# Orders for the whole run in place of periods, and groups of 2, 2, fourteen times 4, 2, 2 sequences

## What is computed

```python
x = x + _L0_xattn_ref(_layernorm(x), ctx, ...)   # 16 heads of 8: q, k, v, rms norm of q and k, softmax, values, projection
x = x + _L0_ffn_ref(_layernorm(x), ...)          # activations and weights rounded; 128 -> 512, convolution over 3 tokens, silu, 512 -> 128
x = x + _L1_xattn_ref(_layernorm(x), ctx, ...)   # one head of 128: softmax(bf . ctx) . ctx, joined with x, 256 -> 128
x = x + _L1_ffn_ref(_layernorm(x), ...)          # 8 experts of 256; every token is taken by every expert
# _L1_ffn_ref, where K = 128 tokens are taken of 128:
#   affinity = softmax(x @ gate_w);  h = silu(x @ Wg[e]) * (x @ Wu[e]);  x_out += affinity[e] * (h @ Wd[e])
```

## Time and profile before

| | us |
|---|---|
| median of 3 runs | 1228.7 |
| lowest, highest | 1226.46, 1229.22 |
| span of the profiled execution | 1219.6 |
| PE busy | 1100.5 |
| DVE busy | 984.3 |
| ACT busy | 826.6 |
| POOL busy | 682.8 |

### The profile page before, as it was taken

The page is one execution under the profiler, slowest core; times in us unless marked ns, Lnnn a source line. Parts: engine busy times, 40 slices in busy tenths (PEclk is TensorE's granted clock), DMA queues, the critical chain, the costliest instruction groups (busy, mean ns, idle before and its releaser), DMA issues.

```text
span 1219.6 us, 27479 instructions
## 1 busy us (share of the span) xinstructions
PE 1100.5 (90%) x9891; PEld 789.6 (65%) x9891; DVE 984.3 (81%) x2728; ACT 826.6 (68%) x1685; POOL 682.8 (56%) x827
## 2 busy tenths in 40 slices
PE   1677778999999899999999999999999998989998
PEld 1544555766767676767757676767767675767775
DVE  3668787989899898989898898989898897877653
ACT  1255375878768686768778686868778686868655
POOL 3212134566565747566575748475575747375775
PEclk9688898999999999999999999999999999999999
DMA  6120212121312113121212112130212022011000
GB/s 207 30 55 20 55 36 56 35 47 38 62 38 56 36 34 56 35 53 32 62 38 57 36 38 53 35 64 21 62 38 60 22 35 48 22 23 26 18 10 9
DMA packets 151396, 53.63 MB, mean 44 GB/s; under 512 B 116832, under 2 KB 150624, under 8 KB 150880
## 3 DMA queue, kind: packets, MB, share of 16 engines
q1 hardware_dynamic: 149248, 47.82, 17.7%
q10 hardware_dynamic: 2016, 4.08, 0.9%
HBM read 24.73 MB, written 4.19 MB: 24 GB/s over the span
## 4 chain that ended last, share of the span: by engine, by line
PE 72%; DVE 12%; SPq 5%; POOL 4%; issue 2%; ACT 2%; DMA 1%; POOLq 0%; DVEq 0%; ACTq 0%
PE py L750 16%; PE pa L601 5%; SPq L444 4%; PE pa L568 4%; PE pg L740 4%; PE pu L740 3%; PE pg L742 3%; PE pg L741 3%; PE pu L741 3%; PE pu L742 3%; PE pa L591 3%; DVE q_st L1155 2%; PE pa L608 2%; PE pb L648 2%; POOL xn L921 2%
## 5 line engine op out<-in xcount | busy, mean ns | idle before, releaser
L962 POOL TENSOR_TENSOR moe<-moe 128x512 f32<-128x512 f32 x256 | 336.3, 1318 | 293.7 <-ACT moe L897 147.8
L750 PE MATMUL py<-wd_s,moe 128*128 128x128 f32 x1856 | 248.7, 278 | 3.9 <-POOL moe L962 3.7
L750 PEld LDWEIGHTS py<-wd_s,moe 128*128 128x128 f32 x1856 | 231.7, 192 | 21.7 <-issue 7.8
L883 ACT ACTIVATE tg<-pg 128x512 f32<-128x512 f32 x232 | 139.7, 602 | 104.7 <-PE pg L742 104.0
L1155 DVE TENSOR_REDUCE q_st<-pa 128x4 f16<-128x480 f32 x256 | 168.4, 658 | 34.8 <-PE pa L568 33.6
L1307 DVE SCALAR_TENSOR_TENSOR moe<-tg,pg 128x512 f32<-128x512 f32 x232 | 157.3, 678 | 32.1 <-ACT tg L883 30.1
L897 ACT ACTIVATE moe<-pu 128x512 f32<-128x512 f32 x232 | 140.4, 605 | 33.7 <-PE pu L742 31.8
L817 ACT ACTIVATE probs<-pa 120x512 f32<-120x512 f32 x256 | 139.8, 605 | 22.3 <-PE pa L591 22.0
L568 PE MATMUL pa<-kbd,qht 128*128 128x480 f16 x256 | 96.4, 377 | 30.7 <-DVE q_st L1155 26.4
L740 PE MATMUL pg<-x4h,wg_h 128*128 128x512 f16 x232 | 88.6, 382 | 16.4 <-DVE moe L1307 16.4
L921 POOL TENSOR_SCALAR xn<-x,lnm,lnr 128x128 f32<-128x128 f32 x192 | 88.3, 473 | 5.2
(11 more groups left out here) (198 smaller groups left out, 2514.4 us busy)
## 6 DMA issues: line engine op xcount, KB each, us to landing
kbd<-kht SPq DMA_DIRECT2D x512, 3.8 KB
xin<-in_x SPq DMA_DIRECT2D x16, 256.0 KB, 2.8
xres<-in_x SPq DMA_DIRECT2D x16, 256.0 KB, 3.0
out_x<-acc SPq DMA_DIRECT2D x16, 256.0 KB, 3.2
ctxt_a<-in_ctx_t SPq DMA_DIRECT2D x16, 240.0 KB, 2.7
ctxt_b<-in_ctx_t SPq DMA_DIRECT2D x16, 240.0 KB, 2.9
ctxn_b<-in_ctx SPq DMA_DIRECT2D x16, 240.0 KB, 3.6
wd_s<-in_wd ACTq DMA_DIRECT2D x1, 1024.0 KB, 9.5
```

The source lines that it names most:

```text
L750: mm = pe.matmul(moe_y(g, e)[:, j, :], hu[:, u % 3, j * S:(j + 1) * S], wd_s[:, u, :], start=(half == 0 and j == 0), stop=(half == 1), ski ...
L883: act.activation(tg[:, u % 2, :], moe_bank("g", g, u)[:, :], ACT.Tanh, scale=0.5 / WSCALE).then_inc(tg_done.sem, 1)
L962: pool.tensor_tensor(hu[:, u % 3, :], gw[:, u % 3, :], us[:, u % 3, :], ALU.mult)\
```

## The change

- **Group sizes.** `SIZES` gives 18 groups: 0 and 1, and 16 and 17, have 2 sequences, the fourteen between them 4. `FIRST[g]` is a group's first sequence. Tiles keep their size; a small group uses the first half of each, so most of its instructions have 256 columns in place of 512. Semaphores that count sequences count by `FIRST` (`Signal.each`).
- **Whole-run orders.** `periods`, `TURNS` and `run_turns` go. `ORDER` has one string of letters per engine for the whole run, and `run` takes for each letter the next step of that stage, whatever the group. A stage of one group may begin between any steps of another.
- **Seven streams.** The max matmuls, their DVE maxima and the second kbd load are a stream of their own, **m**, so that they can run ahead of stage a, into the next group.
- **Finer steps.** q, k and v are three steps, the taps two, the rms and gate steps are single instructions of DVE's row, and POOL's layer norms are split into the roots (`roots`) and the four scalings (`normalise`).
- **kbd.** A small group also takes 32 DMAs, 16 for each of its two sequences.
- **Waits** that periods had made needless are written out, such as those for the last reads of x4h2, q_st2, qht2 and aff by the group two back.
- `UNREAD` is empty. `TAIL = 3` keeps the second banks for groups 15, 16 and 17.

```diff
 B, S, SC, D = 64, 128, 120, 128
-GB = 4
-NG = B // GB
+SIZES = (2, 2) + 14 * (4,) + (2, 2)
+GB = max(SIZES)
+NG = len(SIZES)
+FIRST = tuple(sum(SIZES[:g]) for g in range(NG))
...
-UNREAD = {
-    "wna": {2: 12, 6: 2, 9: 2, 10: 2, 11: 1, 14: 1, 19: 1, 22: 1, 24: 1, 29: 1, 32: 1, 36: 1, 41: 1, 44: 1, 45: 2, 49: 1, 50: 1, 52: 1},
...
+UNREAD = {}
+TAIL = 3
...
     def at(self, g, k=1):
-
-        return g * self.per + k
+        return g * self.per + FIRST[g] * self.each + k
...
-TURNS = {
...
+STAGES = "wnmabdc"
+ORDER = {
+    "sp": (
+        "annnnnnnnmnnnnannmnnbnnbnnmannndnbbnmnnanndncmnbbbnbnnnanmcdnbbbbnnnmannndbbbnbcannmnndnbbbbnnncamdnnnbbbbnn",
...
-            if g >= NG - 3 and u % 2:
+            if g >= NG - TAIL and u % 2:
...
+        def run(engine, do, between=None):
+
+            todo = {stage: iter([(step, g) for g in (range(NG) if stage != "w" else (0,))
+                                 for step in steps_of(engine, stage, g)]) for stage in STAGES}
+            for at, stage in enumerate("".join(ORDER[engine])):
                 if between is not None:
-                    between(kind, at)
-                step = next(steps[stage])
-                do[stage](step, groups[stage])
+                    between(at)
+                step, g = next(todo[stage])
+                do[stage](*step, g)
...
-            def load_kbd(g, half):
-
-                part = slice(2 * half, 2 * half + 2)
-                if later(g):
-                    sp.wait_ge(max_ps.sem, max_ps.at(g - 1, 4 * (2 * half + 2)))
-                for h in range(H):
+            def load_part(g, half):
+                part = slice(0, first_half(g)) if half == 0 else slice(first_half(g), size(g))
+                for h in range(H):
                     rows = slice(h * HD, (h + 1) * HD)
                     sp.dma_start(kbd[rows, part, h, :], kht[rows, part, 0:SC]).then_inc(kbd_in[half][h // HQ].sem, 16)
...
-                    o = moe_bank(what, g, u)
-                    pe.matmul(o[:, :], w_hi[:, us], x4h[:, :], start=True, stop=False)
+                    o = moe_bank(what, g, u)[:, 0:wide]
+                    pe.matmul(o, w_hi[:, us], x4h, start=True, stop=False)
...
-            def normalise(sig, at, n, src, dst):
-
-                pool.tensor_scalar(lnv[:, n, :], mv[:, n, :, 1], EPS_LN, 1.0, ALU.add, ALU.mult).then_inc(sig.sem, 1)
+            def roots(sig, at, i, n):
+
+                pool.tensor_scalar(lnv[:, i, 0:n], mv[:, i, 0:n, 1], EPS_LN, 1.0, ALU.add, ALU.mult).then_inc(sig.sem, 1)
```

More of the change, by code:

```diff
@@ L352, in build_program @@
-        n_steps = ["ln1", "xn1t", "qkv", "rms", "rms_k", "rms_q", "qkht"]
-        a_steps = [("max", 0, c) for c in range(4)]
-        a_steps.append(("stacks", 0))
-        for t in range(GB):
-            steps = [("scores", t, 0), ("max", t + 1, 0), ("scores", t, 1), ("values", t, 0), ("max", t + 1, 1),
-                     ("values", t, 1), ("max", t + 1, 2), ("max", t + 1, 3), ("turn", t), ("stacks", t + 1)]
-            a_steps += [step for step in steps if not (step[0] in ("max", "stacks") and step[1] == GB)]
@@ L359, in build_program @@
-        a_steps += ["ont", "proj"]
-        b_steps = ["ln2", "quant", "xit"]
-        for k in range(KB + 1):
-            steps = [("taps", k - 1), ("fc1", k), ("silu", k - 1)]
-            b_steps += [step for step in steps if 0 <= step[1] < KB]
-        b_steps += [(name, t) for t in range(GB) for name in ("h2t", "hit")] + ["fc2"]
-        d_steps = ["ln3", "xn3t", "bf", "s1", "p1n", "p1t", "oc", "fused", "ln4", "xn4t", "gate"]
-        c_steps = []
-        for u in range(NU):
-            c_steps += [("g", u), ("u", u)] + ([("d", u - 2)] if u >= 2 else [])
@@ new lines, in do_n, with do_m @@
+                    load_part(g, 0)
+            def load_part(g, half):
+                part = slice(0, first_half(g)) if half == 0 else slice(first_half(g), size(g))
+                for h in range(H):
+                    rows = slice(h * HD, (h + 1) * HD)
+                    sp.dma_start(kbd[rows, part, h, :], kht[rows, part, 0:SC]).then_inc(kbd_in[half][h // HQ].sem, 16)
+            def do_m(name, t, c, g):
+                sp.wait_ge(kht_in.sem, kht_in.at(g, 16))
+                if g == 0:
+                    sp.wait_ge(kbd_clear.sem, 1)
+                if later(g):
+                    sp.wait_ge(max_ps.sem, max_ps.at(g - 1, 4 * size(g - 1)))
+                load_part(g, 1)
@@ L690, in do_d @@
                 elif step == "bf":
-                    pe.matmul(pd[:, :], aw1_s[:, :], xn3t[:, :], start=True, stop=True).then_inc(bf_ps.sem, 1)
+                    pe.matmul(pd[:, 0:wide], aw1_s[:, :], xn3t[:, 0:wide], start=True, stop=True).then_inc(bf_ps.sem, 1)
                 elif step == "s1":
-                    for j in range(GB):
+                    for j in seqs:
                         mm = pe.matmul(pd[:, j * SC:(j + 1) * SC], bft[:, j * S:(j + 1) * S], ctxt_b[:, j, :],
```

929 lines of the change are left out of this document (493 added, 436 removed).

## The result

The changed kernel takes 1261.6 us (median of four runs, 1259.12 to 1263.67), the kernel before 1229.0 us beside it; the ratio is 1.0263, with a 95% interval of 1.0234 to 1.0291. The forecast was 1206 us. The profiled execution's span is 1261.5 us, 41.9 more than before.

The account below looks back on a forecast made before the run. PE set the pace from 269 us on, with DVE close behind; before that, chains of short steps did. Head 273, eleven groups 729 and tail 194.5 sum to 1197 us; runs lie 9.1 above the span, so 1206 us, range 1183 to 1238.

Parts of the forecast that it names:

- The turn: Eleven groups between the marks: 2.0 of PE's 3.9 us lost per group go, so 66.3 us each, 729 us.
- The waits named in the earlier trace: PE's waits at the start of a group's turn, 1.48, 1.13 and 0.48 us; the first two were to go.
- next in line is ACT: Near unit 12, ACT's roundings and scaled copies ahead of the tanh make PE wait 0.7 us for g of unit 13.
- Rival 1: The turn is only rearranged: PE still loses 3.9 us a group elsewhere, since DVE leaves little room; 1232 us, chance 0.10.
- Rival 2: ACT comes late for the tanh of units 12 to 14: PE loses 6 us a group, 1254 us, chance 0.15.
- the mark: Start of stage c of sequence 4 (group 2 after, group 1 before): forecast at 273 us, against 269 before.
- The head: Run up to stage c of sequence 4: stage c begins at 148 us, remaining DVE work at 92% takes it to 273.
- the walk: Head's step-by-step issue times: kht at about 33 us, group 1 through SP at 91, second hi_t of group 0 at 110.
- Rival 3: A worse head: without the 95 unread matmuls PE's clock may be 1.2 GHz; mark at 288 us, total 1221, chance 0.08.
- DVE's sum: DVE's busy time over the whole run was to rise by some 20 us.
- The price of small instructions: DVE instructions at 256 columns: two halves cost 0.23 us more than one whole, 13 us for a pair of small groups.
- The tail: Stretch from stage c of sequence 48 to the end: 194.5 us, against 201.1 before.

Follow-up runs that it names:

- the product cut: Changed kernel with GpSimd's product hu = gw * us cut to 8 of up to 512 columns (work left out): 1215.7 us; same cut in the kernel before: 1219.1 us.
- the kernel with the moved steps: Changed kernel with three kinds of steps of VectorE's order moved in each of seven equal turns, nothing left out: 1279.0 us, ratio 1.0449 to the kernel before.
- the clock raised to 0.86: Changed kernel with 112 unread matmuls added between TensorE's steps ahead of the first stage c: 1269.1 us, ratio 1.036 to the kernel before.
- the new order: Changed kernel's groups with whole-run orders of all five engines laid anew, 34 unread matmuls ahead of stage c: 1193.7 us, ratio 0.9723 to the kernel before.

## Why the prediction was wrong, step by step

**The turn (729 us forecast, 768.9 measured): the step that failed.** The waits named in the earlier trace rows went. The step "next in line is ACT", 2.0 us lost a group, named the wrong successor. Next in line was DVE, by longer instructions: every duration was read from a kernel whose order kept DVE's SBUF steps mostly clear of POOL's, and was carried over as if it belonged to the instruction. It belongs to the pair. The lengthening was put at nothing and measured 103 us of DVE's time in place of 18. With the product cut the eleven groups take 742.1 us, so 26.8 of the 39.9 us missed are the product's. Rival 1 named the engine, DVE, but left it 30 us short (1232 us). Rival 2 came within 8 us (1254) and had the sign, with the wrong engine; that is luck.

**Groups 2 and 3.** Here lie 25 of the 39.9 us. The sum took the steady turn from the mark on. Measured are 158.0 us for these two, 147.3 with the product cut and 145.3 in the best order, against 132.6. Every engine has more work in them than in two steady turns: with the cut PE is busy 140.6 us where two of the seven equal turns have 131, and DVE 129.7 where they have 118. The order works further ahead than the old one here, and less is left for the last two of the eleven. The forecast had no such term, and the 14.7 us that stay with the cut are the part of the miss that the product does not explain.

**The head (148 and 273 us forecast, 156.9 and 282.5 measured).** One row of DVE and three of SP's issues of the changed kernel, the latter against the earlier trace rows and the walk built on them:

```profile
20.35 6.99 DVE L1129 TENSOR_SCALAR w_i<-hr 128x512 f16<-128x512 f32 x1
```

```profile
38.52 1.30 SPq L475 DMA_TRANSPOSE kht<-k_hi  x1
...
84.03 10.67 SPq L502 DMA_DIRECT2D kbd<-kht  x16
...
124.91 1.21 SPq L521 DMA_TRANSPOSE hi_t<-hq  x1
```

kht is issued at 38.5 us in place of 33: w_i<-hr takes 6.99 us (0.43 at its other use in this trace), while POOL clears kbd from 20.57 on for 6.49 us. That is one more collision, and it covers the 5 us; it is there with the product cut too. SP's kbd rows of group 1 end at 94.7 (forecast 91). The second hi_t of group 0 is issued at 124.9 (forecast 110), because SP stands still from 98.4 to 109.7 us until hq for the first one is there: the walk took SP to be busy throughout. Stage c starts 9 us late.

From there on the head's sum held: DVE does 115.0 us of work at 92% up to the mark, as forecast, so the whole 9.5 us are the late start. They are not the product's. With the product cut stage c still starts at 155.6 us. The mark then lies at 275.0, but it also lies at 275.0 in the kernel with the moved steps, whose rows are the changed kernel's up to there and which has no cut. So the 7.5 us between 282.5 and 275.0 are no more than two executions of the same rows differ by.

Rival 3 (the clock) came near in its time, 288 us, and not in its cause: with the clock raised to 0.86 the mark did not come earlier (284.5). The Trainium skill's rule that the prediction set beside it (TensorE: Matmul & The Clock Gate, section on loop structure) holds as far as the clock goes, which was 0.82 ahead of stage c against 0.88; it did not set the time.

**DVE's sum.** Forecast 20 us more, measured 75; with the product cut 15, and in the new order 20. The price of small instructions fits these two, though both still hold some 36 us of excess.

**The tail (194.5 forecast, 210.1 measured).** 197.8 with the cut and 198.7 in the new order: the forecast was some 3 us too low. The cut takes 12.3 us off; it also takes 4 off the tail of the kernel before, so some 8 of them are the product's collisions.

Put together: the span came out 64.5 us above the sum of 1197. The cut of the product takes 46.6 of them away (5.7 in the kernel before); 7.5 of the 46.6 stand in the head and may be the scatter told above; the other 17.9 us of the miss are chiefly groups 2 and 3. The new order's span, 258.0 + 734.8 + 198.7 = 1191.5 us, is close to the sum by chance: its head is 15 us shorter than forecast, its turns and tail 10 longer.

## What to carry to other kernels

A duration read from a trace holds for what ran beside it. Where a change moves DVE and POOL against each other, list which DVE instructions have all operands in SBUF and where POOL's stand, and price their meetings: here one cost up to a whole POOL instruction (6.5 us behind the memset), and those with the product cost more than the change was to gain. Then ask who waits behind: two orders with twice the excess of the kernel before were faster than it. Moving single steps here only handed the collisions on (101 us of excess after, 103 before); laying the whole order anew, with the meetings and PE's gaps counted, took 5.3% off, 34 unread matmuls included. And a mark in the head needs more than one execution: it moved by 7.5 us without any change.

## What the runs showed of the hardware

- Which pairs meet. Beside POOL's product of two SBUF tiles (1.26 us), DVE's tensor_scalar, tensor_tensor, scalar_tensor_tensor and f32-to-f16 cast on SBUF end 0.98 to 1.04 us later. Reduce, reciprocal, bn_stats, an operand in PSUM and a 128x1 tensor_scalar do not. The Trainium skill's rule in the section named above (a DVE instruction in a two-port mode or with two SBUF inputs) agrees for the forms that the section names: cast, tensor_scalar, tensor_tensor, tensor_reduce. Reciprocal, bn_stats and the 128x1 form it does not name.
- Beside POOL's memset (0.52 us) the forms split: tensor_scalar takes 0.71 us in place of 0.43 and the cast 0.70, but tensor_tensor and scalar_tensor_tensor keep their 0.69. The same section says that two SBUF inputs collide only with a GpSimd instruction that reads SBUF; a memset reads none.
- Who comes first is not read from the recorded start alone, where the same section gives the ports to the one that starts first. Beside POOL's tensor_scalar with two per-partition scalars DVE kept its time although it started 0.05 us later, and POOL was longer:

```profile
1287.90 2.35 POOL L1064 TENSOR_SCALAR moe<-moe,mv 128x512 f32<-128x512 f32 x1
...
1292.98 2.61 POOL L1064 TENSOR_SCALAR moe<-moe,mv 128x512 f32<-128x512 f32 x1
```

  Beside reduce, which does not collide, it took 2.07 us; beside tensor_scalar and tensor_tensor the 2.35 and 2.61 shown. No run here tells why. The other way round, DVE first by some 0.15 us, the product takes 1.63 us behind tensor_tensor and 1.42 behind tensor_scalar with a per-partition scalar, and its 1.26 behind reduce and the form with a PSUM operand.
- PE's clock fell in the middle of a busy turn: behind two waits of 1.54 and 0.87 us with one max matmul between them, 3.4 us at 1.2 GHz followed, and so in six turns alike.
